# A gather ring of 12 sets of rows in place of 32, a ring of 8 one-hot chunks in place of 7, and staging transposes one gram piece earlier

## The reference

```python
e = jnp.stack([tbl_0[ids[:, 0]], ..., tbl_25[ids[:, 25]]], axis=1)      # (512, 26, 128)
sd = jnp.einsum('bfd,bd->bf', e, dense)
ss = jnp.einsum('bfd,bgd->bfg', e, e)
iu, ju = jnp.triu_indices(26, k=1)
z = jnp.concatenate([dense, sd, ss[:, iu, ju]], axis=1)
h = jnp.concatenate([z, dense], axis=1)
h = jnp.maximum(h @ W_top1 + b_top1, 0.0)     # 512 wide
h = jnp.maximum(h @ W_top2 + b_top2, 0.0)     # 256 wide
y = h @ W_top3
```

## Time and profile before

| what | us |
|---|---|
| median of 3 runs (147.0 to 147.94) | 147.9 |
| the profiled execution | 147.75 |
| its span, first to last instruction | 145.9 |
| PE busy | 91.8 |
| DVE busy | 74.3 |
| POOL busy (64 gathers: 67.8) | 68.5 |
| ACT busy | 61.7 |

### The profile page before, as it was taken

The page is one execution under the profiler, slowest core; times in us unless marked ns, Lnnn a source line. Parts: engine busy times, 40 slices in busy tenths (PEclk is TensorE's granted clock), DMA queues, the critical chain, the costliest instruction groups (busy, mean ns, idle before and its releaser), DMA issues.

```text
span 145.9 us, 3331 instructions
## 1 busy us (share of the span) xinstructions
PE 91.8 (63%) x1420; PEld 75.7 (52%) x1420; DVE 74.3 (51%) x170; ACT 61.7 (42%) x131; POOL 68.5 (47%) x70
## 2 busy tenths in 40 slices
PE   0288999999699963221111001176879978988893
PEld 0256888888488841110100000175768868867791
DVE  1398999999958600000000000049986748576621
ACT  4423928668192850000000000049956768675511
POOL 3787887878787877777777775000000000000000
PEclk9999999999999997555555555555799999999999
DMA  3999949489941211122212212000000000000000
GB/s 61 264 393 364 275 109 313 130 163 380 362 126 44 54 48 46 54 54 54 54 54 54 54 54 53 1 7 4 4 0 4 4 4 0 4 4 0 4 2 1
DMA packets 6850, 13.37 MB, mean 92 GB/s; under 512 B 2354, under 2 KB 3507, under 8 KB 6835
## 3 DMA queue, kind: packets, MB, share of 16 engines
q1 hardware_dynamic: 4112, 8.95, 19.5%
q0 software_dynamic: 2048, 4.20, 10.3%
q10 hardware_dynamic: 674, 0.01, 0.3%
HBM read 13.15 MB, written 0.00 MB: 90 GB/s over the span
## 4 chain that ended last, share of the span: by engine, by line
PE 35%; issue 31%; POOL 15%; DMA 6%; ACT 6%; DVE 5%; DVEq 0%; ACTq 0%
POOL rows L294 15%; PE gram L371 10%; PE hidden L398 6%; DMA rows<-in_tables_gather,idx 5%; PE gram L342 5%; PE second L415 4%; ACT Z L492 4%; DVE Z L568 3%; PE hidden L342 3%; PE stage L325 3%; ACT ET L470 2%; PE hidden L387 1%; DMA idg<-in_ids_gather 1%; PE second L413 1%; PE stage L398 1%
## 5 line engine op out<-in xcount | busy, mean ns | idle before, releaser
L294 POOL DMA_INDIRECT rows<-in_tables_gather,idx x64 | 67.8, 1059 | 20.9 <-issue 19.2
L568 DVE COPY Z<-gram 32x112 f32<-32x112 f32 (+3 forms) x72 | 23.1, 321 | 54.0 <-PE gram L371 53.1
L492 ACT COPY Z<-gram 32x112 f32<-32x112 f32 (+1 forms) x72 | 23.2, 322 | 51.7 <-PE gram L371 50.9
L371 PE MATMUL gram<-ET 128*32 128x27 f32 x1024 | 18.5, 207 | 42.0 <-issue 37.6
L371 PEld LDWEIGHTS gram<-ET 128*32 128x32 f32 x1024 | 14.7, 124 | 46.4 <-issue 42.4
L552 DVE TENSOR_SCALAR onehot<-ids,rowid 128x1024 fp32r<-128x1024 int16 (+1 forms) x48 | 29.1, 662 | 3.6 <-DMA ids<-in_ids_one 2.0
L342 PE MATMUL gram<-onehot,part 128*128 128x512 f32 x80 | 22.3, 431 | 6.6 <-DVE part L558 6.2
L342 PEld LDWEIGHTS gram<-onehot,part 128*128 128x128 f32 x80 | 16.2, 209 | 10.6 <-DVE onehot L552 6.2
L342 PE MATMUL hidden<-onehot,part 128*128 128x512 f32 x80 | 19.8, 397 | 0.6 <-issue 0.6
L342 PEld LDWEIGHTS hidden<-onehot,part 128*128 128x128 f32 x80 | 14.6, 188 | 3.8 <-issue 0.8
L558 DVE TENSOR_TENSOR part<-raw,part 128x1024 fp32r<-128x1024 f32 (+2 forms) x11 | 12.1, 1123 | 2.9 <-ACT part L459 1.3
(11 more groups left out here) (38 smaller groups left out, 39.5 us busy)
## 6 DMA issues: line engine op xcount, KB each, us to landing
raw<-in_tables_one SPq DMA_DIRECT2D x9, 512.0 KB
ids<-in_ids_one SPq DMA_DIRECT2D x4, 256.0 KB, 5.2
rows<-in_tables_gather,idx POOLq DMA_INDIRECT x64
W1s<-in_W_pairs SPq DMA_DIRECT2D x1, 768.0 KB
W1d<-in_W_dense SPq DMA_DIRECT2D x1, 512.0 KB
W2s<-in_W_top SPq DMA_DIRECT2D x1, 512.0 KB
raw<-in_tables_one SPq DMA_DIRECT2D x1, 384.0 KB
ids<-in_ids_one SPq DMA_DIRECT2D x2, 128.0 KB
```

Source lines behind the costliest of these rows:

```text
L294: pool.indirect_dma_start(out=rows[:, m % ROWS_RING, :], out_offset=None, in_=x["tables_gather"], in_offset=bass.IndirectOffsetOnAxis(ap=i ...
L371: last = pe.matmul(gram[p % 2][32 * i:32 * i + 32, NV * j:NV * (j + 1)], ET[:, VP * b:VP * (b + 1)], ETv[:, b, 0:NV], start=True, stop=True)
L492: last = act.copy(dst, src)
L568: last = dve.tensor_copy(dst, src)
```

## The change

Three edits. `ROWS_RING` falls from 8 blocks of 4 gathers to 3 blocks (12 gathers): the buffer `rows` shrinks, the index of a gather in it is taken modulo 12, and the first gather of block n waits, from block 3 on, for the transposes of block n-3 in place of n-8. `RING` goes from 7 to 8 chunks of one-hots. And in the order written for PE and ACT, b8, b9 and b10 stand behind gram pieces 1, 2 and 3 in place of 2, 3 and 4, b11 stands in `SOON` of piece 4 in place of `LATER` of piece 4, and b12 in `SOON` of piece 5 in place of `LATER` of piece 5. b13, b14 and b15 stay. The two stage banks go on alternating in the same order of blocks.

```diff
--- before.py
+++ after.py
@@ -36,14 +36,14 @@
 RAW = 3
 
 SIDE = [[0], [1, 2], [3, 4], [5, 6], [7, 8], [9]]
-RING = 7
+RING = 8
 
 
 BS = 32
 NB = B // BS
 GB = BS * NM // P
 NG = NB * GB
-ROWS_RING = 8 * GB
+ROWS_RING = 3 * GB
 
 
 
@@ -200,8 +200,8 @@
         AMID = {(0, 7): ["dense"], (1, 3): ["b0"], (2, 1): ["b1"], (2, 5): ["b2"], (3, 1): ["b3"],
                 (3, 6): ["b4"], (4, 3): ["b5"], (4, 7): ["b6"], (5, 7): ["b7"]}
 
-        SOON = {2: ["b8"], 3: ["b9"], 4: ["b10"]}
-        LATER = {4: ["b11"], 5: ["b12", "b13"], 6: ["b14"], 7: ["b15"]}
+        SOON = {1: ["b8"], 2: ["b9"], 3: ["b10"], 4: ["b11"], 5: ["b12"]}
+        LATER = {5: ["b13"], 6: ["b14"], 7: ["b15"]}
         STAGED = [s for g, k in sorted(AMID) for s in AMID[g, k]] + [s for n in range(NP) for s in SOON.get(n, []) + LATER.get(n, [])]
 
         def bank_of(name):
```

## The result

The changed kernel takes 133.31 us (132.15 to 135.49) where the kernel before took 147.87 us in the same comparison: a ratio of 0.901, 95% interval 0.8955 to 0.9067. That is faster, as forecast, 2.1 us under the 135.4 us predicted. The profiled execution of after took 132.72 us with a span of 130.9 us. The kernel before took about 147 us in some jobs (a job is a set of runs of both kernels taken together on one chip) and about 108.5 us in others, two chips having both, so each experiment is read against the kernel before of its own job, and several of them say only what happens where the hole of the earlier trace rows is absent.

A forecast was written before the change was run, and what follows sets the result against it. PE's issue, held back by gathers in flight, was taken as the bound. Span 145.9 - 24.8 - 0.7 = 120.4 us gave 122.2 us in time; plus 13.2 us for the hole's return, 135.4 us; range 120 to 150 us.

The forecast's parts named there:

- the hole: In gram piece 0, PE's issue gaps until 95.82 us, blamed on gathers in flight; would end at 70.9 us, gain 24.8 us.
- the rule that was weighed against the forecast: Engine and DMA ports are disjoint, so the gathers are innocent of the hole and it stays: 147.2 us.
- gain from the moved transposes: b8 to b12 transposed earlier, piece 5 no longer waiting for ACT: taken as 0.7 us gain.
- The first term: Gram pieces 0 and 1 end at 73.7 us in place of 98.51 us, gain 24.8 us.
- r: PE's recovery to full rate after a gather block's landing in pieces 2 to 6; bounds 0 and 4.5 us, taken as 0.
- Rival 3: In pieces 2 to 6 the hole comes back with 4.5 us recovery after each of five blocks: 157.9 us; chance 0.16.
- rival 1: The hole ends early and doesn't come back in pieces 2 to 6: 122.2 us; chance 0.28.
- POOL's first pause: POOL stops after gather 43, at about 65 us, for some 9 us.
- The later cycles: After piece 2, transposes, gathers, landing and rest of each piece take 7.9 + r us, where now 5.9 us.
- clock term: No term given for the clock, since the granted clock is 0.5 at the end of both.
- The one-hot chunk: RING 7 to 8 in the look-ups: taken as 0, bound 0.4 us, hidden by PE.
- Rival 2: The hole isn't due to the gathers and lasts to 95.8 us; only 0.7 us saved: 147.2 us; chance 0.18.

## Why the prediction was right

**What held.** The sum named the right bound and the right mechanism: gathers in flight hold back the gram's matmuls, the ring of 12 stops the gathers in the hole, the hole ends early, and it comes back beside the later blocks. The run without late gathers shows the first of these; the timelines of after show the others in pieces 2 to 5. In piece 6, which the sum took for the fifth, it doesn't come back. The matmuls themselves don't get slower. In the page's groups the gram matmul takes 207 ns on the mean in after, and 199 ns in the run without late gathers where no hole was (207 ns too in the kernel before):

```profile
L371 PE MATMUL gram<-ET 128*32 128x27 f32 x1024 | 17.0, 207 | 25.8 <-issue 12.8
```

```profile
L371 PE MATMUL gram<-ET 128*32 128x27 f32 x1024 | 12.4, 199 | 8.0 <-issue 4.8
```

It is their issue that stops. That also settles the rule that was weighed against the forecast. The Trainium skill (SBUF — State Buffer, SBUF: two separate sides) says that DMA and compute ports are disjoint. Nothing here contradicts it for a matmul's own duration; but the step from it to "the gathers are innocent of the hole" does not hold, by 147.76 against 114.12 us. On the fetch of instructions the DMA view adds that the one instruction packet of the earlier trace rows lies between 53.5 and 54 us, and the next behind 97 us, when the full rate has been back for over 1 us.

**The terms, in us of span.** The forecast was 133.55 (135.4 less 1.85), measured 130.9.

| term | predicted | measured in after |
|---|---|---|
| pieces 0 and 1 done | 73.7 | 67.84 + 2.72 = 70.6 |
| end of pieces 0 and 1 to end of piece 2 | 8.6 | 78.30 - 70.56 = 7.7 |
| end of piece 2 to end of piece 6 | 31.6 | 110.65 - 78.30 = 32.35 |
| gain from the moved transposes | 0.7, taken off apart | in the rows above |
| end of piece 6 to the end | 20.3 | 20.3 |

The first term was too large by 3.1 us. Block 10's issue ended 1.7 us later than forecast (66.85 for 65.16 us), but the recovery of 4.5 us, taken from the one hole in the trace, was far too long. Counted from the traffic's end (67.8 us in after) it is nothing in after, 0.4 us in the run without late gathers (62.04 less 61.6 us) and 1.2 us in the second profile of the changed kernel. Before it PE had crawled for 5, 9 and 14 us, and for 43 us in the kernel before. The recovery grows with how long the crawl has lasted, by these four rows. That supports the choice of r near 0 for the later blocks and speaks against using 4.5 us for the first. Rival 3 (r = 4.5 us, 157.9 us) falls by the same numbers, and rival 1 (no return, 122.2 us) by the timelines of pieces 2 to 5. POOL's first pause, put at some 9 us, took 4.6 us and 6.1 us in the two profiles.

One reading was off and changes no term: the 40 and 32 that the argument calls gathers in the earlier trace rows are POOL's instructions by window. By POOL's timeline 34 gathers start before 52.6 us and 30 behind it.

**The later cycles** came to 7.9, 7.5 and 7.6 us for pieces 3, 4 and 5 (ends at 86.20, 93.72 and 101.30 us) against 7.9 us. The cycle of piece 6 took 9.35 us, and for another reason than forecast: piece 6 waited for no gathers, but for the layers behind piece 5. The sum has no clock term for them. The granted clock was 1.00 while piece 5 crawled (96.88 to 100.29 us); at about 101 us it fell to its lower level (1.2 GHz) and stayed there to about 107.9 us, where the layers behind piece 4 had the upper (2.4 GHz). The windows (length, busy us and count of PE, PEld, DVE, ACT, POOL, then clock, DMA share, GB/s) and PE's timeline:

```profile
96.88:100.29 3.41, 1.01 (x42) 0.87 (x42) 0.95 (x3) 0.69 (x2) 1.89 (x2) 1.00 0.24 58
...
102.28:108.09 5.81, 5.81 (x24) 5.22 (x24) 3.10 (x11) 2.41 (x7) 3.77 (x4) 0.52 0.15 38
```

```profile
94.14 1.03 PE L415 MATMUL second<-W2s,h1T 128*128 128x256 f32 x4
...
103.00 2.07 PE L415 MATMUL second<-W2s,h1T 128*128 128x256 f32 x4
...
105.30 1.49 PE L398 MATMUL hidden<-Z,W1s 128*128 128x128 f32 x6
```

From 102.28 us (layer 2 begins) to 108.09 us (transposes of b13) the layers take 5.8 us, and those of piece 3 from 86.72 to 89.99 us 3.3 us. So these layers took 2.5 us longer at the lower clock. Not all of it is a loss of the cycle: at the upper clock piece 6 would have met block 15's gathers, and its cycle, taken as those of pieces 3 to 5, would have been 7.7 us, so the net cost is about 1.7 us (an estimate from these rows). That the crawl of piece 5 brought the fall isn't shown: piece 3 crawled as long (81.70 to 85.28 us), and the clock stayed at 1.00 behind it, to 89.99 us. A total within 2% rests here on a first term too large by 3.1 us, and behind it on shorter cycles and a missing clock term that nearly cancel.

**The transposes.** Piece 5 starts at 96.88 us with no wait for ACT, as said. The wait of 0.73 us before piece 5 is gone; PE's wait for ACT's ET copies by L470 remains before pieces 6, 7 and 8, 0.68 us each. The one-hot chunk was given 0: no run here separates it. Nor do the runs part the ring from the order where the hole is; that the ring's pauses bring the gain is read from the timelines of after.

**Where the argument had luck.** Rival 2 said that the hole isn't due to the gathers. The runs show late gathers as necessary for it (without them it ends at 62 us), but not as sufficient: the same gathers beside the same matmuls give 108.5 us on the same chips at other times. I read a single execution and took its hole as a property of the kernel. The three runs shown agreed within 0.7%, which made it look settled. In a comparison without the hole the answer would have been "no change", or 0.7% at best, and my range began at 120 us. What the other condition is, I can't say. Its traces show the same pace of gathers and about the same DMA shares (0.20 and 0.23), and no event ends the gaps.

## What to carry to other kernels

A stretch in which PE's matmuls are very short and its gaps read "issue" while POOL's gathers run is worth one experiment: leave the gathers out and see whether the gaps end with them. If they do, short pauses of the gathers behind each dense piece bring back part of the time at once (10% here), because the crawl ended within 1.2 us of the traffic's end where it had lasted 5 to 14 us, and 4.5 us behind it where it had lasted 43 us; while pauses that make rows late cost more than they save (4% here where there was no crawl). And repeat the kernel before in several jobs before believing a hole that no event explains: here it was worth 39 us of 148, and of nine jobs it was there in three and absent in five; the ninth had one run of 146.98 us among nine whose cause isn't known.

## What the hardware showed beyond expectation

- One program on one chip takes 108 us or 147 us, by the job; chips 6 and 10 had both.
- ACT, with nothing to wait for, stood still for 8.2 us beside running gathers and went on 1.6 us behind their last traffic; POOL stood still for 3.0 us at the same time. It happened in one of two profiles of the changed kernel. It looks like the same hold on another engine's instructions, but this is argued from the times alone.
- A pause in the gathers restores the full rate of short matmuls at or soon behind the last landing (0 to 1.2 us), and new gathers take it away again: 1.6 us behind their start in piece 2, and after 34 to 47 matmuls in each piece from 2 to 5. Where it sets in it is thus no slow build-up over 50 us of look-ups.
